# Two roundings, one chunk's taps and the last maxima dealt out anew at the end of a fused two-layer block

## The reference

```python
def act_quant(x):
    scale = 127.0 / jnp.clip(jnp.max(jnp.abs(x), axis=-1, keepdims=True), 1e-05)
    return jnp.clip(jnp.round(x * scale), -128, 127) / scale
...
h = bit_linear(x, w1)                      # 512 -> 2048, weights rounded to -1, 0, 1
h = depthwise_conv1d(h.transpose(0, 2, 1), conv_w, conv_b)   # 3 taps along the tokens
h = h.transpose(0, 2, 1)
h = jax.nn.silu(h)
return bit_linear(h, w2)                   # 2048 -> 512
...
x = x + jnp.tanh(g_ffn[1]) * _L1_ffn_ref(_layernorm(x, axis=-1), ...)
```

## Time and profile before

| | us |
|---|---|
| median of 3 runs | 1915.39 (1914.12 to 1917.5) |
| the profiled execution | 1913.22 |
| its span in the trace | 1911.4 |
| VectorE busy | 1718.4 (90%) |
| TensorE busy | 1578.7 (83%) |
| ScalarE busy | 1461.6 (76%) |
| GpSimd busy | 578.9 (30%) |

### The profile page before, as it was taken

One profiled execution on the slowest core, in us unless ns is written; L12 is line 12 of the kernel. 1 busy time (PEld: TensorE's weight loads), 2 busy tenths in 40 slices (PEclk: granted clock), 3 DMA queues, 4 the chain that ended last, 5 costly groups with the idle time before them and its releaser, 6 DMA issues.

```text
span 1911.4 us, 24370 instructions
## 1 busy us (share of the span) xinstructions
PE 1578.7 (83%) x9414; PEld 710.9 (37%) x9481; DVE 1718.4 (90%) x2634; ACT 1461.6 (76%) x1076; POOL 578.9 (30%) x469
## 2 busy tenths in 40 slices
PE   7778965698657975787489978999999987999987
PEld 4222211132111321232134435666666652444443
DVE  6999999999999999989789967999999758999997
ACT  4899999999999999999846645545555437887880
POOL 1000000000000000000011126666666644998991
PEclk9999999999999999999989989999999999999998
DMA  5000200020000012100348773333333111122212
GB/s 207 1 22 15 76 12 1 23 76 19 6 1 1 17 39 100 55 12 12 129 160 318 269 198 120 107 107 103 111 116 96 45 56 39 45 78 77 67 56 77
DMA packets 123270, 146.54 MB, mean 77 GB/s; under 512 B 31375, under 2 KB 80655, under 8 KB 122771
## 3 DMA queue, kind: packets, MB, share of 16 engines
q1 hardware_dynamic: 123154, 144.98, 23.0%
HBM read 87.55 MB, written 51.77 MB: 73 GB/s over the span
## 4 chain that ended last, share of the span: by engine, by line
ACT 44%; PE 33%; DVE 13%; POOL 4%; issue 4%; DMA 2%; SPq 0%; DVEq 0%; ACTq 0%; POOLq 0%
ACT unit L595 41%; PE psum L1114 7%; PE psum L1796 5%; PE psum L1830 5%; PE psum L1782 3%; DVE unit L499 2%; POOL h L1971 2%; PE psum L1806 2%; PE psum L1823 2%; PE psum L1853 2%; DVE psum L1562 2%; DVE psum L1567 1%; POOL hidden L1988 1%; PE psum L1815 1%; PE psum L1885 1%
## 5 line engine op out<-in xcount | busy, mean ns | idle before, releaser
L595 ACT ACTIVATE unit<-unit 128x4096 f32<-128x4096 f32 x244 | 857.5, 3613 | 1.0 <-DVE unit L499 0.8
L499 DVE TENSOR_SCALAR unit<-feat_proj,text_proj 128x1024 f32<-128x1024 f32 x976 | 667.8, 747 | 50.5 <-PE psum L747 47.5
L747 PE MATMUL psum<-unit,w_pad 128*32 128x512 f32 x3904 | 470.6, 600 | 222.9 <-ACT unit L595 222.7
L747 PEld LDWEIGHTS psum<-unit,w_pad 128*32 128x32 f32 x3904 | 102.2, 109 | 537.9 <-ACT unit L595 380.9
L1853 PE MATMUL psum<-xq_block,w_q 128*128 128x512 bf16 x489 | 119.7, 385 | 15.8 <-ACT h L1729 11.1
L1971 POOL TENSOR_TENSOR h<-h,arow 128x512 f32<-128x512 f32 x104 | 125.8, 1232 | 19.5 <-ACT h L1729 19.5
L650 PE MATMUL psum<-xnT,W_sb 128*128 128x512 f32 x256 | 123.4, 610 | 1.9 <-ACT xnT L549 1.9
L798 POOL TENSOR_SCALAR rstd<-mv 128x8 f32<-128x8 f32 (+1 forms) x5 | 1.7, 334 | 403.4 <-DVE mv L250 403.4
L1704 ACT ACTIVATE scores<-scores 128x1024 f32<-128x1024 f32 x32 | 33.9, 1059 | 113.9 <-POOL scores L1957 113.9
L1988 POOL TENSOR_TENSOR hidden<-hidden,srow 128x2048 f32<-128x2048 f32 x28 | 114.4, 4084 | 10.0 <-DVE hidden_q L1597 9.7
L1796 PE MATMUL psum<-xnT_c,wq_sb 128*128 128x256 f32 x512 | 115.7, 379 | 1.4 <-ACT xnT_c L1691 1.4
(11 more groups left out here) (263 smaller groups left out, 2688.1 us busy)
## 6 DMA issues: line engine op xcount, KB each, us to landing
h_scratch<-h SPq DMA_DIRECT2D x44, 512.0 KB, 3.3
hin<-h_scratch SPq DMA_DIRECT2D x32, 704.0 KB, 4.7
xin<-in_x SPq DMA_DIRECT2D x8, 1024.0 KB, 6.5
x<-in_x SPq DMA_DIRECT2D x16, 512.0 KB, 3.6
x_scratch<-x SPq DMA_DIRECT2D x32, 256.0 KB, 2.0
x3in<-x_scratch SPq DMA_DIRECT2D x31, 256.0 KB, 4.0
out_rows<-x3in SPq DMA_DIRECT2D x28, 256.0 KB, 2.0
xnT_scratch<-xnT SPq DMA_DIRECT2D x6, 1024.0 KB, 5.7
```

Of the source, the lines that this page charges most:

```text
L499: ins = ve.tensor_scalar(units[:, n % 3, k, :], FP[:, bi % 2, k, :], TP[:, k, n:n + 1], None, ALU.add)
L595: ac.activation(units[:, n % 3], units[:, n % 3], ACT.Tanh).then_inc(unit_tanh, 1)
L747: mm = te.matmul(psum[k * TG:(k + 1) * TG, 3 + 2 * grp + half, :], w_pad[:, k, TG - 1 - tt:2 * TG - 1 - tt], units[:, n % 3, k, half * BAN ...
```

## The change

- ScalarE, not VectorE, rounds tiles 26 and 27 (`LAST_ROUND`, block `NF - 2`), in two passes each, between the Silus of block 7. GpSimd scales tile 27 without waiting for the rounding of tile 26.
- TensorE does the taps of chunk 15 in the last block (`LAST_TAPS`). ScalarE prepares the three diagonal matrices during the attention half (`last_tap_weights`).
- The last half's maxima, chunks 8 to 15, are taken in two parts: 8 to 11 in slot 416, 12 to 15 where the whole half was.
- The product of tile 27 goes to bank 1 (`NEXT_BANK`) and no longer waits for the addition of tile 26.
- The additions of tiles 26 and 27, of tile 28 and of the sequences' ends move into `last_block`, between its scalings and roundings.
- SyncE loads the rows of tiles 29, 30 and 31 together after the store of tile 27, and stores the ends before tile 28.

```diff
@@ slots and helpers
+    LAST_TAPS_AT, LAST_TAPS_EVERY = 1420, 108
+    MOVED2 = {(HS, NF - 2): (575, 617, 680, 715), (OUT, NF - 2): (703, 728, 857, 923), (HMAX, NF - 1): (322, 416)}
+
+    def slots2(slots, f):
+        return MOVED2.get((slots, f), slots)
...
+    LAST_TAPS, LAST_PTAP = (15,), (430,)
+
+    def by_tensor(f, c):
+        return c in PE_TAPS or f == NF - 1 and c in LAST_TAPS
...
+    LAST_ROUND, LAST_HRA, LAST_HRB = (2, 3), (700, 740), (705, 745)
...
-    END_BANK, LAST_BANK = 0, (1, 2, 3, 7)
+    LOADED_AT = {NT - TPK - 1: range(NT - TPK + 1, NT), **{NT - 1 - i: () for i in range(TPK)}}
+    END_BANK, NEXT_BANK, PART_BANK, LAST_BANK = 0, 1, 2, (5, 2, 3, 7)
@@ VectorE
+                last = n == 2 * NF - 1
+                if last:
+                    V.wait_ge(raw_copied, len(GP_MID) * NF)
+                    V.wait_ge(silu2_done, max(nth(f, c, SILU, CHUNKS) for c in range(HALF, HALF + HALF // 2)))
...
+                if last:
+                    V.wait_ge(hmax_step, 2 * NF)
+                    ve.tensor_tensor(hm[:, 0, :], hm[:, 0, :], psum[:, PART_BANK, :], ALU.max).then_inc(hmax_step, 1)
...
             for f, i, n in before_last(of(q, HROUND, VE_ROUND)):
+                if f == NF - 2 and i > 1:
+                    continue
...
-                if t < NT - TPK - 1:
+                if t < NT - TPK - 2:
                     add_rows(f, i, OUT_BANK)
@@ VectorE, last_block
-            ve.tensor_reduce(hm[:, 1, :], H2[f % 2][:, HALF // 2:].rearrange("p g t r -> p t g r"), AX.XY, ALU.max,
-                             apply_absolute_value=True).then_inc(hmax_step, 1)
+            ve.tensor_reduce(psum[:, PART_BANK, :], H2[f % 2][:, HALF // 2 + HALF // 4:].rearrange("p g t r -> p t g r"), AX.XY,
+                             ALU.max, apply_absolute_value=True).then_inc(hmax_step, 1)
...
+            add_rows(f - 1, TPK - 2, OUT_BANK)
             V.wait_ge(spread_mm, 2 * NF + 1)
...
-            add_rows(f - 1, TPK - 1, OUT_BANK)
             for i in range(TPK):
...
-            for i in range(TPK - 1):
+                if i == 0:
+                    add_rows(f - 1, TPK - 1, NEXT_BANK)
+                if i == 1:
+                    V.wait_ge(spread_mm, 2 * NF + 3)
+                    V.wait_ge(x3in_loaded[3], TERN_LOADS + 16 * NF)
+                    ve.scalar_tensor_tensor(out=x3end[0:NB, :], in0=psum[0:NB, END_BANK, :], scalar=hs4[0:NB, 2:3],
+                                            in1=x3end[0:NB, :], op0=ALU.mult, op1=ALU.add).then_inc(hmax_step, 1)
+                if i >= 2:
+                    add_rows(f, i - 2, LAST_BANK[i - 2])
+            for i in range(TPK - 2, TPK):
                 add_rows(f, i, LAST_BANK[i])
-            V.wait_ge(spread_mm, 2 * NF + 3)
...
@@ ScalarE
+                ac.activation(tapd[:, len(PE_TAPS) + j, k, :], ident[:, :], ACT.Copy, scale=cw_sb[:, c, k:k + 1])
...
-            for f, i, n in before_last(of(q, HRA, AC_ROUND)):
+            for f, i, n in rounds_by_scalar(q, HRA, LAST_HRA):
@@ TensorE
-            for f, c, n in of(q, PTAP, PE_TAPS):
-                j = PE_TAPS.index(c)
+            for f, c, j in tensor_taps(q):
...
-                T.wait_ge(bank_read[OUT_BANK], ATT_TURNS[OUT_BANK])
-                T.wait_ge(out_done, t)
+                bank = OUT_BANK if t < NT - TPK - 1 else NEXT_BANK
+                if bank == OUT_BANK:
+                    T.wait_ge(bank_read[OUT_BANK], ATT_TURNS[OUT_BANK])
+                    T.wait_ge(out_done, t)
+                else:
+                    T.wait_ge(raw_copied, len(GP_MID) * NF)
@@ GpSimd
-                if i - 1 in VE_ROUND:
+                if i - 1 in VE_ROUND and not (f == NF - 2 and i - 1 in LAST_ROUND):
@@ SyncE
-                if t == NT - 1:
-                    S.wait_ge(hmax_step, 2 * NF + 1 + 10)
-                    sp.dma_start(out[ends, :], x3end[0:NB, :]).then_inc(out_stored[0], 16)
+                if t == NT - TPK:
+                    S.wait_ge(hmax_step, LAST_STEPS + 12)
+                    sp.dma_start(out[ends, :], x3end[0:NB, :]).then_inc(x3_ends_stored, 16)
                 store_rows(t)
-                if t + 2 < NT:
-                    load_rows(t + 2)
+                for r in LOADED_AT.get(t, (t + 2,)):
+                    load_rows(r)
```

More of the change, by code:

```diff
@@ L1389, in at1, with tensor_taps @@
             yield g, i, g * TPG + i
+    MOVED2 = {(HS, NF - 2): (575, 617, 680, 715), (OUT, NF - 2): (703, 728, 857, 923), (HMAX, NF - 1): (322, 416)}
+    def slots2(slots, f):
+        return MOVED2.get((slots, f), slots)
     def at2(q, slots):
-        for f, c in hit(q - OFF2, slots, N2, NF):
+        if slots not in placed2:
+            placed2[slots] = {}
+            for f in range(NF):
+                for c, s in enumerate(slots2(slots, f)):
+                    placed2[slots].setdefault(s + f * N2 + OFF2, []).append((f, c))
+        for f, c in placed2[slots].get(q, ()):
             yield f, c, f * len(slots) + c
+    placed2 = {}
     def of(q, slots, chunks):
         for f, j, n in at2(q, slots):
-            yield f, chunks[j], n
+            if not (chunks == VE_TAPS and by_tensor(f, chunks[j])):
+                yield f, chunks[j], n
+    def tensor_taps(q):
+        for f, c, n in of(q, PTAP, PE_TAPS):
+            yield f, c, PE_TAPS.index(c)
+        for j, s in enumerate(LAST_PTAP):
+            if q == OFF2 + N2 * (NF - 1) + s:
+                yield NF - 1, LAST_TAPS[j], len(PE_TAPS) + j
     def turns(*uses):
@@ L1429, in edged, with tap_turn @@
         return max(2, 2 * f + c // HALF + 1)
+    LAST_TAPS, LAST_PTAP = (15,), (430,)
+    def by_tensor(f, c):
+        return c in PE_TAPS or f == NF - 1 and c in LAST_TAPS
+    def tap_turn(f, c):
+        at = dict(zip(PE_TAPS, PTAP))
+        if f == NF - 1:
+            at.update(zip(LAST_TAPS, LAST_PTAP))
+        return SEL_SUMS + f * len(PE_TAPS) + sum(1 for s in at.values() if s <= at[c])
     def upto(f, c, chunks):
@@ L1435, in nth @@
         at = slots[chunks.index(c)]
-        return f * len(chunks) + sum(1 for s in slots if s <= at)
+        return f * len(chunks) + sum(1 for s, d in zip(slots, chunks)
+                                     if s <= at and not (chunks == VE_TAPS and by_tensor(f, d)))
     def of_half(f, k, slots, chunks):
-        return max(nth(f, c, slots, chunks) for c in chunks if c // HALF == k)
+        return max(nth(f, c, slots, chunks) for c in chunks
+                   if c // HALF == k and not (chunks == VE_TAPS and by_tensor(f, c)))
     def scaled_by(engine, f, c):
```

76 lines of the change are left out of this document (45 added, 31 removed).

## The result

| | before | changed |
|---|---|---|
| median of six executions, us | 1915.45 (1912.17 to 1918.14) | 1909.32 (1907.61 to 1911.58) |
| ratio of times | | 0.9971, 95% interval 0.9959 to 0.9983 |
| profiled execution, us (span) | 1913.22 (1911.4) | 1911.58 (1909.8) |
| R, start of the last block's first maxima, us | 1854.23 | 1858.00 |
| R to the end of the span, us | 57.17 | 51.80 |

The change made the kernel faster: by 6.1 us by the two medians, by 5.6 by the recorded ratio, whose interval gives 3.3 to 7.9. The forecast of 1911.3 was 2.0 us above the measured median, and the range of 1908.6 to 1915.6 held it.

The account below looks back on a forecast made before the run. VectorE was the path at the end, waiting in order for others' deliveries. Gains of 3.6 us up to the spread scales and 0.5 after took 1913.22 to 1909.1; 2.2 more for the median gave 1911.3, range 1908.6 to 1915.6.

Parts of the forecast that it names:

- What is late next is TensorE: Before the last transposes, VectorE's maxima are combined at 1879.3, 1.9 us ahead of TensorE, which becomes the late one.
- P: Moment when TensorE is free for the last transposes: 1879.7 at full clock, 1881.2 with the low clock charged.
- rival 1: TensorE's clock does not fall at all in its pause before the taps: gain 5.6 us, 1909.8; chance 0.20.
- S: Moment when TensorE's spread scales are ready: 1888.08 before, forecast 1884.5 after, a gain of 3.6 us.
- the low clock at tile 26: TensorE's clock falls to 0.50 after its pause, as before, costing 1.48 us ahead of the last transposes.
- The spread and the transposes: At the end of the last block, TensorE's spread of the scales takes 1.16 us at full clock instead of 2.07.
- Rival (2): The clock falls again at the transposes: +0.9 at the spread, +0.4 at the transposes, gain 2.8, 1912.6; chance 0.17.
- (3): ScalarE becomes the bound, its passes meeting another wait and stretching: P 2.2 later, gain 1.9, 1913.5; chance 0.09.
- (5): The change doesn't do what it says; the order of rows was said to show it does; no chance given.
- rival (4): TensorE stays at the low clock from taps to transposes: slower, 1920.6; chance 0.09 together with anything unseen.
- The edge copy on GpSimd: After chunk 15's taps, ahead of the last part of the maxima, GpSimd's copy takes 1.12 us.
- What splitting the maxima is worth: Halving the second half's 4.33 us maxima gains nothing by itself; 4.33 for the last part would cost 0.2.

Follow-up runs that it names:

- the filled kernel: The kernel before with products nobody reads put in TensorE's two last pauses, one ahead of tile 27 and two ahead of the last transposes: 1911.94 us.

## Why the prediction was right, and where a term was off

*What is late next is TensorE.* It was. The transposes began with the end of the tiles, and VectorE waited 1.59 us for them. In steps from R, forecast and measured: taps +15.9 and +15.96; P at full clock +25.5 and +25.52; the maxima combined, at full clock (1878.2 in rival 1), +24.0 and +24.24; S at full clock +28.8 and +28.84; the last addition 19.55 and 19.61 behind S. The queue of ScalarE, read row by row from durations of the old trace, gave the start of the taps to 0.1 us, with the wait of 1.3 for GpSimd (measured 1.32).

*The term that was mis-sized.* It is the low clock at tile 26, charged with 1.48 us "again". The clock did not fall there in either profile of the changed kernel, in which the taps in front of that tile began behind pauses of 2.70 and 1.01 us, so the term measured 0, and the gain in the profiles was 5.4 where the forecast had 4.1, close to the 5.6 of rival (1) and outside the forecast's own 3.0 to 5.2. That the median still came within 2.0 us of the forecast is no proof of the sum: the range was wide enough for both cases. My step was "up to 1870 TensorE does the same as now, so I charge it again". The runs show that what TensorE did before doesn't settle it. One execution of the changed kernel had the low clock on tile 25 (5.30), the other nowhere after R. The kernel before had it at tile 26 once (5.09) and not the second time (3.61). Over all six profiles in which tile 26 came behind the same pause of 3.14 or 3.15 us, it fell in three; tile 25, behind 2.23 us, was slow in two of twelve. A fall of the clock seen once is a chance to be shared between cases, not a term.

*The spread and the transposes.* The forecast of 1.16 at full clock came true (1.16), and the filled kernel shows the mechanism by itself: 1.2 or 0.4 us, by the execution that it is held against. Rival (2), a second fall there, occurred in neither profile of the changed kernel.

*The rivals (3) to (5).* ScalarE did become the bound, but at the price that the sum already held; no further wait came on top. Moving its passes won 2.7 us of M: the sum had charged this order correctly, but the prediction did not see it as a thing to avoid. The low clock throughout, rival (4), didn't come. The edge copy on GpSimd took 0.20, not 1.12, and either way TensorE came later. The three diagonal matrices took ScalarE 0.38 to 0.42 us each, and nothing waited for them; that they cost nothing, as the prediction took it, can't be seen beside R's scatter of 5 us.

*What splitting the maxima is worth.* I wrote "nothing by itself here", and 0.2 at 4.33 for the last part. That was reckoned for the low clock, where TensorE would come 1.5 us later, a case that no run shows; without it the split was worth 0.63. This follows from the same mis-sized term.

*Where the gain came from.* The sum was taken over the whole change, so it could not show that the moves make 3.0 to 3.7 us and the title's three edits 1.7: rounding by ScalarE 0.9, split maxima 0.63, the taps +0.5 in a run with a fall of the clock and, by estimate, -0.4 without. The single parts overlap and need not add up.

*The median.* M gives 5.4 or 4.7 us, the medians 6.1 and the recorded ratio 5.6, with an interval of 3.3 to 7.9; the difference of up to 1.4 is within that and isn't explained further.

## What to carry to other kernels

When the engine on the path waits in order behind others, write down each neighbour's queue row by row from the old trace and add the new work where it really stands; this gave the starts of the taps, the transposes and the last addition to 0.1 us. Then ask which instruction in that queue the next bound hangs on, and let it go first: the same passes, queued a few steps later, shortened the end by another 2.7 us in the one profile. And look at a load that lands late before building around it: what stands ahead of it in its queue may be a transfer that uses one engine of sixteen.

## What the runs showed of the hardware

- One 127-row store kept 1 of 16 DMA engines at 17 GB/s, and the load queued behind it landed after 12.92 us; with the store split into 112 and 15 rows the load landed after 2.9 us. The load's own issue (0.50 to 4.23 us behind the four such stores) did not tell: all four landed after 12.9.
- TensorE's clock is not the same function of the work in each execution. The changed kernel's repeat had it at 0.50 on tile 25, and its first profile at 1.00 all the way from R to the end. The stretch of the repeat (columns as above):
```profile
1864.00:1866.00 2.00, 2.00 (x6) 0.64 (x5) 0.02 (x1) 2.00 (x3) 2.00 (x1) 0.50 0.07 15
```
The level of 0.50 is 1.2 GHz. "TensorE: Matmul & The Clock Gate", Part 1, in the Trainium skill says that the monitor behind this clock runs freely and does not start anew with the kernel. That would fit the 5.30 and 3.61 us of the same tile, but no run here shows the monitor itself.
- One execution of the kernel with later passes took 5631 us. TensorE was busy for 99% of its span at a granted clock shown as 1.00, each fp8 product with a mean of 1103 ns instead of 379, and the other products likewise, while VectorE's busy time was as ever (1731.3 us against 1717.5). The same kernel took 1904.6 to 1910.4 in ten other executions. What slowed TensorE stays open. The groups of one line (count, busy us, mean ns, idle before), of that execution and of the second run of the same kernel:
```profile
L1958 PE MATMUL psum<-w_q,hidden_q 128*128 128x512 fp8e4 x448 | 375.1, 1103 | 0.9 <-DVE x3in L1666 0.9
```
```profile
L1958 PE MATMUL psum<-w_q,hidden_q 128*128 128x512 fp8e4 x448 | 101.1, 379 | 6.7 <-ACT hidden_q L1825 3.2 <-DVE x3in L1666 2.2
```
The same 448 products, with almost three times the mean time and 3.7 times the busy time.
